# Cross-attention and a two-of-eight expert block on one core: the choice of experts through DRAM, and new orders for all engines

## The reference, cut to what matters

```python
# x, ctx: (32, 128, 128)
q, k, v = LN(x) @ wq + bq, ctx @ wk + bk, ctx @ wv + bv      # 16 heads of 8
o = softmax((q k^T / sqrt(8)) v, over the 8 of a head)        # no softmax over keys
x = x + o @ wo^T + bo
t = rms(LN(x)) * norm_w
probs = softmax(t @ gate^T)                                   # 8 experts
top 2, weights normalised
h1 = t @ w1^T + 2 * (t @ a1_e^T) @ b1_e^T                     # for each chosen e, rank 16
h3 = t @ w3^T + 2 * (t @ a3_e^T) @ b3_e^T
act = silu(h1) * h3                                           # 512 wide
x = x + sum over the two e of weight * (act @ w2^T + 2 * (act @ a2_e^T) @ b2_e^T)
```

## Time and profile before

| | us |
|---|---|
| median of 3 runs | 319.68 (318.21 to 324.47) |
| the profiled execution | 318.86 |
| its span, first to last instruction | 316.8 |
| PE busy | 300.6 (95%) |
| DVE, ACT, POOL busy | 224.4, 198.2, 189.2 |
| mean granted TensorE clock | 0.989 |
| first matmul of the experts' base (L559) | at 31.27 |
| loop blocks 1 to 7 start | at 70.46 (block 1), 142.22 (3), 249.60 (6), 281.70 (7) |
| last matmul of w2 (L621) | at 309.94 |

### The profile page before, as it was taken

One profiled execution on the slowest core, in us unless ns is written; L12 is line 12 of the kernel. 1 busy time (PEld: TensorE's weight loads), 2 busy tenths in 40 slices (PEclk: granted clock), 3 DMA queues, 4 the chain that ended last, 5 costly groups with the idle time before them and its releaser, 6 DMA issues. The chain is left out here.

```text
span 316.8 us, 4667 instructions
## 1 busy us (share of the span) xinstructions
PE 300.6 (95%) x1569; PEld 243.6 (77%) x1569; DVE 224.4 (71%) x621; ACT 198.2 (63%) x337; POOL 189.2 (60%) x171
## 2 busy tenths in 40 slices
PE   6778999999999999999999999999999999998994
PEld 5546787768787888888887888888887878786873
DVE  3767984895669756895769756895669756963375
ACT  2456956478647777478647767478747746863521
POOL 3363459927991588627892588717861489226920
PEclk9997999999999999999999999999999999999997
DMA  5720020000200020000200020000000000000000
GB/s 158 273 59 10 1 66 2 1 0 3 99 0 2 0 66 36 0 3 0 86 15 2 0 68 33 0 2 1 5 30 0 1 2 34 1 2 0 33 0 33
DMA packets 5063, 8.95 MB, mean 28 GB/s; under 512 B 560, under 2 KB 1840, under 8 KB 5040
## 3 DMA queue, kind: packets, MB, share of 16 engines
q1 hardware_dynamic: 4320, 7.54, 7.3%
q10 hardware_dynamic: 720, 1.12, 1.0%
HBM read 6.56 MB, written 2.10 MB: 27 GB/s over the span
## 5 line engine op out<-in xcount | busy, mean ns | idle before, releaser
L849 ACT ACTIVATE silu<-h_ps 128x512 f32<-128x512 f32 x64 | 38.2, 597 | 28.2 <-PE h_ps L573 26.2
L1131 DVE TENSOR_TENSOR act_first<-silu,h_ps 128x512 f32<-128x512 f32 x32 | 21.9, 686 | 42.1 <-ACT silu L849 25.1
L573 PE MATMUL h_ps<-um_hi,b_hi 128*128 128x512 f32 x128 | 51.3, 401 | 0.1
L573 PE MATMUL h_ps<-um_lo,b_hi 128*128 128x512 f32 x128 | 50.7, 396 | 0.1
L573 PE MATMUL h_ps<-um_hi,b_lo 128*128 128x512 f32 x128 | 50.6, 395 | 0.0
L1354 POOL TENSOR_TENSOR heads<-e_o,rec_o 128x512 f32<-128x512 f32 (+1 forms) x9 | 14.8, 1645 | 45.0 <-DVE rec_o L1040 45.0
L1383 POOL TENSOR_TENSOR scaled<-act_second,ratio 128x512 f32<-128x512 f32 x24 | 31.3, 1308 | 17.0 <-DVE act_second L1131 16.8
L1131 DVE TENSOR_TENSOR act_second<-silu,h_ps 128x512 f32<-128x512 f32 x32 | 21.3, 683 | 14.6 <-PE h_ps L573 13.8
L573 PEld LDWEIGHTS h_ps<-um_lo,b_hi 128*128 128x128 f32 x128 | 24.0, 188 | 6.2 <-DVE um_lo L1229 0.6
L573 PEld LDWEIGHTS h_ps<-um_hi,b_hi 128*128 128x128 f32 x128 | 24.1, 188 | 5.8 <-DVE act_first L1131 0.4
L573 PEld LDWEIGHTS h_ps<-um_hi,b_lo 128*128 128x128 f32 x128 | 24.1, 189 | 5.4
(11 more groups left out here) (273 smaller groups left out, 810.4 us busy)
## 6 DMA issues: line engine op xcount, KB each, us to landing
x_in<-in_x_dram SPq DMA_DIRECT2D x7, 256.0 KB, 2.9
ctx_in<-in_ctx_t_dram SPq DMA_DIRECT2D x7, 256.0 KB, 3.2
out_dram<-y SPq DMA_DIRECT2D x7, 256.0 KB, 2.0
act_second<-in_hidden_w_dram SPq DMA_DIRECT2D x1, 512.0 KB, 6.1
act_second<-in_lora_w_dram ACTq DMA_DIRECT2D x1, 512.0 KB, 6.0
v_parts<-in_down_w_dram SPq DMA_DIRECT2D x1, 512.0 KB, 5.8
attn_sb<-in_attn_w_dram SPq DMA_DIRECT2D x1, 260.5 KB, 5.7
ctx_in<-in_ctx_t_dram ACTq DMA_DIRECT2D x2, 128.0 KB, 4.4
```

Source lines behind the costliest of these rows:

```text
L573: mm = nc.tensor.matmul((h1_ps, h3_ps)[s][n % 2][:], b13[w][:, s, c * P:(c + 1) * P], um[k][m][:, s, :], start=False, stop=(i == 2), skip_ ...
L849: nc.scalar.activation(silu[:, n % SILU_RING, :], h1_ps[n % 2][:], ACT.Silu).then_inc(silu_done.sem, 1)
L1131: nc.vector.tensor_tensor((act_first, act_second)[k][:, c, :], silu[:, n % SILU_RING, :], h3_ps[n % 2][:], ALU.mult).then_inc(act_done.sem, 1)
```

## The change

The choice of experts of blocks 1 to 7 no longer goes through PE. DVE writes one tile `choice` (12 columns: for 4 tiles the two indices as floats and the gap), SP sends it to DRAM as one row of 1536 numbers and reads this row back into all 128 partitions (`chosen`). A partition compares the indices with the number of its own expert (`row_expert_sb`, a new input); ACT takes exp of the gaps right from `chosen`. Block 0 keeps the old way. The factor 2 (`LORA_SCALE`) moves from the spread into `mask_u` and `v_part`, which become scalar_tensor_tensor of the same size.

Besides, the lists of all engines are laid out anew: block 0 and the last block are taken out of the loop and have lists of their own, and inside the loop the order changes. One semaphore per weight takes the place of the counted `w_hi_ready` and `w_lo_ready`; the load of `lora_w` moves from ACT's queue to SP's. The order of chunks in `a2_product` and `w2_product` is free per block.

```diff
+            def spread_choice(n):
+                sp.wait_ge(choice_done.sem, choice_done.of(n))
+                sp.dma_start(choice_dram[n % 2].rearrange("(p c) -> p c", c=CHOICE), choice[:])\
+                    .then_inc(choice_out.sem, 16)
+                sp.wait_ge(choice_out.sem, choice_out.of(n))
+                if n > 1:
+                    sp.wait_ge(masks_done.sem, masks_done.of(n - 1))
+                    sp.wait_ge(ratio_done.sem, ratio_done.of(n - 1))
+                sp.dma_start(chosen[:], choice_dram[n % 2].partition_broadcast(P)).then_inc(chosen_in.sem, 16)
...
             for b in range(BLOCKS):
                 if b + 3 < BLOCKS:
                     load_x(b + 3)
                     load_ctx(b + 3)
                 if b > 0:
                     store(b - 1)
+                if b + 1 < BLOCKS:
+                    spread_choice(b + 1)
...
-            def spread_masks(n):
-            def turn_ratio(n):
...
-                elif n == 0:
-                    pe.wait_ge(ratio_done.sem, ratio_done.of(b))
                 else:
-                    pe.wait_ge(masks_done.sem, masks_done.of(b))
+                    pe.wait_ge(silu_done.sem, silu_done.of(b - 1, 7 + n))
...
+            for b in range(1, LAST):
+                early = b + 2 < BLOCKS
+                hidden(b, 0)
+                hidden(b, 1)
+                if early:
+                    keys_values(b + 2, 0)
+                    turn_x(b + 2)
+                turn_heads(b + 1)
+                hidden(b, 2)
+                if early:
+                    keys_values(b + 2, 1)
+                project(b + 1)
+                hidden(b, 3)
+                b2_product(b - 1)
+                if early:
+                    keys_times_values(b + 2)
+                    queries(b + 2)
+                hidden(b, 4)
+                tail(b - 1)
+                turn_tok(b + 1)
+                hidden(b, 5, (1,))
+                gate(b + 1)
+                if early:
+                    attention_out(b + 2)
+                hidden(b, 5, (0,))
+                hidden(b, 6)
+                hidden(b, 7)
+                a2_product(b, 1, 1)
+                a2_product(b, 0, 1)
+                a2_product(b, 0, 0)
+                lora_in(b + 1, 0)
+                w2_product(b, 0)
+                lora_in(b + 1, 1)
+                a2_product(b, 2, 1)
+                w2_product(b, 1)
+                a2_product(b, 1, 0)
+                a2_product(b, 2, 0)
+                w2_product(b, 2)
+                w2_product(b, 3)
+                a2_product(b, 3, 1)
+                a2_product(b, 3, 0)
...
+                silu_step(b, 4)
+                tok_turned(b + 1)
+                if b + 3 < BLOCKS:
+                    ctx_high(b + 3)
+                b_high(b, 0)
+                z_high(b, 0)
+                silu_step(b, 5)
+                silu_step(b, 6)
+                silu_step(b, 7)
+                b_high(b, 1)
+                exp_gap(b + 1)
+                exp_ratio(b + 1)
+                z_high(b, 1)
+                b_high(b, 2)
+                z_high(b, 2)
+                if early:
+                    exp_o(b + 2)
+                um_high(b + 1, 0)
+                um_high(b + 1, 1)
...
+            def choose(n):
+                ve.wait_ge(top_l_done.sem, top_l_done.of(n))
+                for t in range(TILES):
+                    op = nc.vector.max_index(top_i[:, t, :], top_l[:, t, :], logits[:, t, :])
+                op.then_inc(top_i_done.sem, 1)
+                if n > 1:
+                    ve.wait_ge(choice_out.sem, choice_out.of(n - 1))
+                    ve.wait_ge(e_gap_done.sem, e_gap_done.of(n - 1))
+                nc.vector.tensor_tensor(choice[:, TOP * TILES:], top_l[:, :, 1], top_l[:, :, 0], ALU.subtract)\
+                    .then_inc(gap_done.sem, 1)
+                ve.wait_ge(gap_done.sem, gap_done.of(n))
+                ve.wait_ge(top_i_done.sem, top_i_done.of(n))
+                nc.vector.tensor_copy(choice[:, 0:TOP * TILES].rearrange("p (k t) -> p t k", k=TOP), top_i[:, :, 0:TOP])\
+                    .then_inc(choice_done.sem, 1)
+
+            def mask(n, k):
+                ve.wait_ge(chosen_in.sem, chosen_in.of(n))
+                dst = masks[n % 2][:, k, :].rearrange("p (t c) -> p t c", t=TILES)
+                if k == 0:
+                    ve.wait_ge(row_expert_in, 16)
+                    nc.vector.tensor_scalar(dst, chosen_part(0), row_expert_sb[:, 0:1], None, ALU.is_equal)\
+                        .then_inc(masks_done.sem, 1)
...
+                act_step(b, 4)
+                top_logits(b + 1)
+                choose(b + 1)
+                if early:
+                    top_of_o(b + 2)
+                tok_low(b + 1)
+                if early:
+                    shift_o(b + 2)
+                act_step(b, 5)
+                act_step(b, 6)
+                act_step(b, 7)
+                scale_last(b)
+                b_low(b, 1)
+                total(b, 2)
+                total(b, 3)
+                mask(b + 1, 0)
+                z_low(b, 1)
+                mask_u(b + 1, 0)
+                z_low(b, 2)
+                b_low(b, 2)
+                mask(b + 1, 1)
+                um_low(b + 1)
+                mask_u(b + 1, 1)
...
+                total_first(b)
+                b_low(b)
+                z_low(b)
+                scale_step(b, 2)
                 if b + 3 < BLOCKS:
+                    ctx_low(b + 3)
                     rstd_x(b + 3)
-                    ctx_low(b + 3)
-                scale_step(b, 2)
                 if early:
                     norm_heads(b + 2)
...
+            b2_product(LAST - 1)
+            a2_product(LAST, 0, 1)
+            a2_product(LAST, 1, 1)
+            a2_product(LAST, 2, 1)
+            a2_product(LAST, 3, 1)
+            w2_product(LAST, 0)
+            a2_product(LAST, 1, 0)
+            tail(LAST - 1)
+            a2_product(LAST, 0, 0)
+            a2_product(LAST, 2, 0)
+            a2_product(LAST, 3, 0)
+            w2_product(LAST, 1)
+            w2_product(LAST, 2)
+            w2_product(LAST, 3)
```

More of the change, by code:

```diff
@@ L749, in _, with last_b2 @@
-            for i in range(2):
+            def last_b2(i):
                 pe.wait_ge(last_v_hi, i + 1)
@@ L761, in _ @@
                 mm.then_inc(last_y_mm, 1)
+            pe.wait_ge(scrap_ready, 1)
+            for _ in range(WARM):
+                nc.tensor.matmul(pair_a[1][:, 0:P], scrap[:], scrap[:], start=True, stop=True)
+            keys_values_ahead(0, 0)
+            keys_values_ahead(0, 1)
+            turn_x(0, 0)
+            turn_x(0, 1)
+            queries(0, 0)
+            keys_times_values(0, 0)
+            keys_times_values(0, 1)
+            attention_out(0, 0)
+            queries(0, 1)
@@ new lines, in _ @@
+            attention_out(0, 1)
+            keys_values_ahead(1, 0)
+            keys_values_ahead(1, 1)
+            turn_heads(0, 0)
+            turn_heads(0, 1)
+            project(0, 0)
+            turn_x(1)
+            project(0, 1)
+            keys_times_values(1)
+            queries(1)
+            turn_tok(0, 0)
+            gate(0, 0)
+            turn_tok(0, 1)
+            gate(0, 1)
+            attention_out(1)
+            lora_in(0, 0)
+            lora_in(0, 1)
+            first_masks(0)
@@ new lines, in _ @@
+            first_masks(1)
+            first_base(1, 1)
+            first_base(0, 0)
+            first_ratio()
+            first_base(0, 1)
+            keys_values(2, 0)
+            first_base(1, 0)
+            hidden(0, 0)
+            hidden(0, 1)
+            turn_heads(1)
+            turn_x(2)
+            project(1)
+            keys_values(2, 1)
+            queries(2)
+            hidden(0, 2)
+            keys_times_values(2)
+            hidden(0, 3)
+            hidden(0, 4)
+            turn_tok(1)
@@ new lines, in _ @@
+            total(0, 2)
+            scale_last(0)
+            z_low(0, 1)
+            total(0, 3)
+            b_low(0, 1)
+            mask(1, 0)
+            z_low(0, 2)
+            b_low(0, 2)
+            mask_u(1, 0)
+            mask(1, 1)
+            um_low(1)
+            mask_u(1, 1)
+            sum_exp(2)
+            v_part(0, 0)
+            first_weight(1)
+            v_part(0, 1)
+            for b in range(1, LAST):
+                early = b + 2 < BLOCKS
+                act_step(b, 0)
+                if early:
+                    keys_values(b + 2, 0)
+                act_step(b, 1)
+                residual(b + 1)
+                if early:
+                    keys_values(b + 2, 1)
+                moments_x1(b + 1)
+                if early:
+                    mask_ktv(b + 2)
+                act_step(b, 2)
+                act_step(b, 3)
+                if b + 3 < BLOCKS:
+                    moments_x(b + 3)
+                finish(b - 1)
+                act_step(b, 4)
+                top_logits(b + 1)
+                choose(b + 1)
```

(37 more changed lines are left out.)

749 lines of the change are left out of this document (375 added, 374 removed).

## The result

| | before | after |
|---|---|---|
| median of the runs | 320.45 us | 349.89 us (346.50 to 351.56) |
| ratio, 95% interval | | 1.093 (1.080 to 1.106) |
| profiled execution, span | 318.86, 316.8 | 348.37, 346.6 |
| first matmul of the base | 31.27 | 37.79 |
| block 1 starts | 70.46 | 79.12 |

Where executions of one kernel lay more than 1.5% apart, the ratio is of the quicker ones. The forecast was 321, range 308 to 336. It went the way of rival (b), and beyond its 335. Of the 29.8 us by which the span grew, 8.7 stand ahead of block 1, 22.5 in blocks 1 to 6, and the last block gave 1.4 back.

What follows compares the result with a forecast made beforehand. PE was taken to bound the loop, never waiting in block 3. Terms -6.7 + 7.5 + 4.2 - 2.3 - 0.7 = +2.0 on 318.86 gave 320.9, stated as 321; own range 315 to 327, with rivals 308 to 336.

Steps and rivals of the forecast that it cites:

- rival (b): In the loop DVE's small copy also waits, for POOL's z_lo; PE waits 3.8 us a block: 335 us, chance 0.23.
- What PE no longer does: Blocks 1 to 7: spread's transposing matmuls and the e_gap turns leave PE, 0.96 us a block, -6.7 us.
- The path through DRAM: choice out to DRAM 2.0 us, chosen back 4.5, with waits 6.6 (5 to 12); just in time for mask 0.
- The time of the choice: On the block's clock DVE reaches gap at 21.35 us; it waits for POOL's b_lo until 23.0, 1.5 us late.
- the stop of the forecast: PE waits before hidden 7 for act 5: 1.5 us in blocks 1 to 4, 0.9 and 0.6 after, +7.5.
- the small copy: DVE's copy behind gap, taken as 0.2 us; its waiting for POOL's z_lo was left to rival (b).
- Blocks 1 to 6, added up: Change foreseen for the span of blocks 1 to 6 together: +5.2 us.
- Block 0 and the start: Both taken as 0; bounds -2.5 to +3 for block 0, -2 to +1.5 for the start.
- The prediction's own sign for this: If the start moves by over 3 us, the zero taken for it was wrong.
- The tail: End of blocks 1 to 4: DVE and POOL take turns, z_low of chunk 2 late by 1.05 us, +4.2 together.
- The last block: b2 of block 6 and its tail move behind hidden 7 and the v_lo wait goes: -2.3 us.
- Rival (c): chosen lands late (9.5 us instead of 4.5): 332 us; or milder, masks reading 48-byte steps take twice 0.6; chance 0.08.

Runs made afterwards that it cites:

- run 3: Changed kernel with both the gap and the copy of the indices on ACT instead of DVE: 316.03 us, ratio 0.987 to the kernel before.
- run 1: Changed kernel with only the copy of top_i into choice moved from DVE to ACT: 322.18 us, ratio 1.012 to the kernel before.
- run 4: Changed kernel with gap and copy still on DVE but behind act 5, blocks 1 to 6: 337.85 us, ratio 1.054 to the kernel before.
- run 12: Separate kernel without the computation: 26 small DVE operations, each beside one POOL operation, to see which wait; no overall time given.
- run 7: Changed kernel with POOL's low parts of W13 and B13 in the start waiting for tok: 346.06 us, ratio 1.082 to the kernel before.
- run 8: run 3 plus the start wait of run 7, and den and w_first of block 0 computed earlier on DVE: 316.03 us, ratio 0.988.
- run 10: run 9 with DVE's tail reordered so that both z_low and b_low of chunk 3 precede mask_u: 314.83 us, ratio 0.983.
- run 9: run 3 with changed start, ACT's ratio after the last z_high, both z_low before mask 0; block 0: scale_mask early, z_low before scale_last: 317.01 us, 0.992.
- run 5: Changed kernel with POOL's b_low and z_low of chunks 0 and 1 each cut into two 512-column operations: 321.57 us, ratio 1.004.
- run 6: run 3 with PE made to wait for POOL's scaled before hidden 7, blocks 1 to 6: 333.3 to 340.7 us, ratio 1.051.

## Why the prediction was wrong, step by step

- **What PE no longer does: right in sign, low in size.** 0.96 us a block foreseen, 1.5 measured where nothing keeps PE waiting (block 5 of run 3). The two turnings' own steps are 0.8 of it. The rest is spread over steps that are shorter in the new order, 0.35 of it at the product of the queries, and was not tested by itself.
- **The path through DRAM: right.** 4.5 us taken for the way back, 4.0 measured; 2.0 for the way out, 1.4 measured. For DVE it arrives in time: in run 1 mask 0 follows 2.5 us behind it, in run 3 1.6. Not foreseen was that ACT's exp of the ratio idles 0.2 to 1.7 us for `chosen` in most blocks of runs 1 and 3. Run 4 shows the price when the choice leaves late.
- **The time of the choice: right.** Gap was reached 21.07 us into block 2 (139.69 - 118.62) where 21.35 was worked out, and it waited for b_lo as said: 1.7 us. Run 1, which leaves this wait alone, has the stop of the forecast (1.2 us).
- **The step that failed: the small copy took no part in the sum.** "That case is a rival below", because no row showed such a copy. The nearest row was there: a four-element tensor_scalar with one input waited in the earlier trace rows. A one-input copy waits in the same way (run 12), and the step of PE rose from the 1.57 of run 1 to 3.91. The rival's 2.3 us a block was exact; giving it 0.23 was the misjudgement. The Trainium skill's rule ("SBUF — State Buffer", section "SBUF: two separate sides") told the right side, and here the trace agrees: all three small copies of run 12 waited 1.8 us.
- **What stood in no case: the clock.** The rival said 335 and forgot what a stop of that length does to TensorE: 43 slow matmuls, 8.5 us in blocks 1 to 6. In block 3 before, the clock is 1.00, and PE never stops for more than 1.0 us in the loop. In blocks 1 to 6 of run 1, stops of 1.2 us and less brought no slow matmul.
- **Blocks 1 to 6, added up.** +5.2 foreseen; the copy's 6 x 2.3 and the clock's 8.5 come on top, the 4.2 of the tail doesn't show: 23.3, and 22.5 were measured.
- **Block 0 and the start: wrong.** Taken as 0, bounds -4.5 to +4.5 together; measured +8.7, of which 6.5 stand ahead of the first base and 2.1 in block 0. The prediction's own sign for this, a start that moves by over 3 us, came. In the start there are two causes. One is the tok collision, the mechanism of the loop in a place where I had looked at DMAs only. The other is that in this execution PE ran at a lower clock early on. Windows from 8 to 17 us, kernel after and then run 1, whose start is the same code:

```profile
8.00:17.00 9.00, 8.07 (x31) 6.51 (x32) 3.83 (x16) 2.06 (x5) 0.01 (x1) 0.65 0.69 240
```

```profile
8.00:17.00 9.00, 7.09 (x38) 5.35 (x38) 6.29 (x22) 3.50 (x10) 2.15 (x5) 1.00 0.70 237
```

  The base began at 37.79 in the one and at 34.03 in the other, so 3.8 of the 6.5 go with the clock of that execution; why it differs stays open. The collision is worth 3.1 us at the low clock (run 7, 0.66 in the same window, base at 34.69) and 2.0 at the full one (runs 8 and 10, bases at 32.07 and 31.84, against runs 1 and 3, 34.03 and 33.91): with the full clock only one of the two tok operations meets POOL, and they take 2.36 instead of 4.66. The two causes overlap and can't be added.

  In block 0 PE stops for 3.75 us for z_lo, with 8 slow matmuls behind. DVE waits four times ahead of it: gap 0.92, copy 2.32, scaled 2.85, z_lo 1.74. But the first two aren't what makes z_lo late, since in run 3, where both are gone from DVE, the stop is still this:

```profile
65.87 0.50 PE L680 MATMUL odd_ps<-z_hi,w2a_hi 128*128 128x512 f32 x1 [3.60 <-DVE z_lo L1327]
```

  It is scaled and z_lo themselves, behind POOL's masks and b_lo. With scale_mask early and z_low ahead of scale_last (run 9) the stop is 1.9, with POOL's halves (run 5) 2.7.
- **The tail: right in size where it can be seen.** 1.05 us a block foreseen, 0.9 in blocks 1 to 4 of run 3 against its block 5. In the kernel after, behind the long stop, PE's steps show no such wait.
- **The last block: right in kind.** -2.3 foreseen, -1.4 measured: PE stops twice for b_lo there, 1.06 and 0.73 us.
- **Rival (c):** the transfer wasn't late. The reads of `chosen` in steps of 48 bytes do cost something: mask 1 takes 1.14 us (two-input operations of this size 0.68), ACT's exp of the ratio 1.15 where the copy it replaces took 0.58; mask 0, with one input, 0.69. PE waits for none of it alone, except in run 4: in run 10 mask 1 (1.16) stands right ahead of um_lo, for which PE waits 0.43, but ACT's um_hi, which um_lo needs as well, ends at the same moment (176.94).
- **Two slips of arithmetic.** 128 x 6 KB are 768 KB, not 786, so the upper price of the way back is 9.3 us, not 9.5. And 320.9 with the 0.8 between execution and median is 321.7, so the sum says 322, not 321. Neither decides anything.

That the new orders alone, with the choice still going through PE, would have been faster or slower was not tried.

## What to carry to other kernels

A small operation isn't cheap for being small: if it is a copy, a tensor_scalar, a tensor_tensor or a scalar_tensor_tensor on DVE with all its inputs in SBUF, its price here was the rest of whatever POOL was doing. Before one is put into a list, look at what POOL runs at that moment, and let ACT do it, or give it an input in PSUM, or cut POOL's long operation in two. When a rival rests on a behaviour that a neighbouring row already shows, put it into the sum. And when a sum has a stop of PE of some 3 us in it, add a case in which the matmuls behind it run at the lower clock. Last, when a time agrees with a forecast, add up its parts before you believe the account: run 1 agreed by errors that cancel.

## What the runs showed of the hardware

- DVE's reciprocal of SBUF data (0.20 us) passes beside POOL; copy, cast, tensor_scalar and scalar_tensor_tensor don't (1.8 us, 8 elements; run 12).
- The wait is for one operation: 1.85 and 2.31 us beside POOL operations of 1024 columns (kernel after), 0.74 and 1.22 beside halves (run 5), with POOL's next operation following at once in both.
- In blocks 1 to 6 the granted clock fell behind every stop of PE of 3.4 or 3.5 us (nine: four in the kernel after, four in run 7, one in run 6), and behind both of 3.0; behind two of four of 2.9; not behind one of 3.3 (run 4), nor behind any of 2.8 and less. Elsewhere it fell behind shorter ones: 8 slow matmuls behind 1.9 us in block 0 of runs 9 and 10, 5 behind 1.06 and 0.72 us, close together, in the last block of run 10, where run 1 has the same two stops and none. So the length of the stop isn't all that decides; what else does was not found.
- In the kernel after, the first slow step came 0.6 to 1.0 us after PE had resumed (146.38 to 147.42 in block 2), and 5 to 12 matmuls took 0.43 us each.
